# Output held by tokens, activations as the stationary operand, and the first experts' products in the last part of attention

## The reference

```python
x = L0_attn_x
xn = _layernorm(x, axis=-1)
x = x + _L0_attn_ref(xn, ...) + _L0_ffn_ref(xn, ...)
```

```python
g = jnp.einsum('th,eih->tei', x, w_gate_proj)     # 32 experts, inner size 96
u = jnp.einsum('th,eih->tei', x, w_up_proj)
h = jax.nn.silu(g) * u
h = h * masked_w[:, :, None]
out = jnp.einsum('tei,ehi->th', h, w_down_proj)
```

## Time and profile before

| | |
|---|---|
| median of 3 runs | 1143.94 us (1143.56 to 1144.35) |
| the profiled execution | 1144.08 us |
| its span, first to last instruction | 1142.3 us, mean granted clock 0.994 |
| TensorE matmul busy | 1106.8 us (97%), 7360 matmuls |
| TensorE weight loads busy | 911.9 us (80%), 7360 loads |
| VectorE, ScalarE, GpSimd busy | 739.5, 635.2, 490.8 us |
| moved by DMA | 67.85 MB, 59 GB/s over the span |

### The profile page before, as it was taken

How to read it: one execution, slowest core, us unless ns; L and a number is a source line. 1 busy time by engine, 2 the same in 40 slices (tenths; PEclk the granted TensorE clock), 3 DMA queues, 4 the chain that set the end, 5 groups by cost and what they waited for, 6 DMA issues and landing times. The chain is left out here.

```text
span 1142.3 us, 22436 instructions
## 1 busy us (share of the span) xinstructions
PE 1106.8 (97%) x7360; PEld 911.9 (80%) x7360; DVE 739.5 (65%) x1556; ACT 635.2 (56%) x1285; POOL 490.8 (43%) x384
## 2 busy tenths in 40 slices
PE   6989999999999999999999999899999999999997
PEld 3668888888888888888888887688888878888885
DVE  6878778678688687687787765454444445444444
ACT  3575766766766767667766676443434333343332
POOL 1265456466466456446546552033333332333332
PEclk9999999999999999999999999899999999999999
DMA  6100000000000000010000021273333334433332
GB/s 221 56 19 19 3 18 20 1 18 18 0 17 19 0 18 18 0 36 0 0 18 0 1 66 30 84 222 110 115 110 115 110 107 131 118 117 110 115 105 92
DMA packets 26309, 67.85 MB, mean 59 GB/s; under 512 B 3028, under 2 KB 9428, under 8 KB 26264
## 3 DMA queue, kind: packets, MB, share of 16 engines
q1 hardware_dynamic: 26120, 67.24, 19.5%
q10 hardware_dynamic: 144, 0.07, 0.0%
HBM read 62.82 MB, written 4.47 MB: 59 GB/s over the span
## 5 line engine op out<-in xcount | busy, mean ns | idle before, releaser
L838 ACT ACTIVATE prob<-ps_s,nm 128x128 f32<-128x128 f32 (+7 forms) x256 | 189.5, 740 | 164.8 <-DVE nm L998 162.9
L1436 POOL TENSOR_TENSOR hl<-hf,hh 128x512 fp32r<-128x512 f32 x96 | 123.4, 1286 | 295.4 <-ACT hh L1373 295.4
L998 DVE CUSTOM_DVE_ANT_0 ps_s<-ps_s,causal 128x128 f32<-128x128 f32 (+7 forms) x256 | 195.5, 764 | 55.0 <-PE ps_s L653 47.5
L664 PE MATMUL ps_t<-ident,prob 128*128 128x128 f32 x1152 | 177.5, 275 | 4.3 <-ACT pt L848 3.0
L664 PEld LDWEIGHTS ps_t<-ident,prob 128*128 128x128 f32 x1152 | 136.5, 140 | 30.4 <-issue 11.4
L679 PE MATMUL ps_o<-pt,kvn 128*64 128x128 f32 x2304 | 154.0, 278 | 0.5 <-DVE pt L1007 0.4
L679 PEld LDWEIGHTS ps_o<-pt,kvn 128*64 128x64 f32 x2304 | 123.2, 136 | 33.3 <-issue 21.3
L1405 DVE TENSOR_TENSOR gs<-gs,routing 128x512 f32<-128x512 f32 x64 | 44.3, 692 | 137.8 <-ACT gs L1369 137.8
L1007 DVE COPY pt<-ps_t 128x128 f32<-128x128 f32 (+2 forms) x192 | 102.0, 531 | 48.3 <-PE ps_t L664 46.4
L1373 ACT ACTIVATE hh<-hf 128x512 fp32r<-128x512 f32 x96 | 60.7, 633 | 121.6 <-DVE hf L1410 121.6
L1369 ACT ACTIVATE gs<-ps_g 128x512 f32<-128x512 f32 x96 | 57.4, 598 | 121.4 <-PE ps_g L1328 121.4
(11 more groups left out here) (291 smaller groups left out, 2560.2 us busy)
## 6 DMA issues: line engine op xcount, KB each, us to landing
routing<-wT_scratch SPq DMA_DIRECT2D x34, 256.0 KB, 3.7
raw_a<-in_e SPq DMA_DIRECT2D x17, 384.0 KB, 3.1
cosv<-in_e SPq DMA_DIRECT2D x17, 384.0 KB, 3.0
sinv<-wT_scratch SPq DMA_DIRECT2D x17, 384.0 KB, 3.6
raw<-in_e SPq DMA_DIRECT2D x17, 384.0 KB, 3.0
routing<-wT_scratch SPq DMA_DIRECT2D x16, 384.0 KB, 3.3
raw_a<-in_a SPq DMA_DIRECT2D x8, 512.0 KB, 3.3
raw_b<-in_b SPq DMA_DIRECT2D x8, 480.0 KB, 3.8
```

Source lines behind the costliest of these rows:

```text
L664: mm = nc.tensor.transpose(ps_t[x][:, at * P:(at + 1) * P], prob[t % 2][e][:, j * P:(j + 1) * P], ident[:, :])
L838: nc.scalar.activation(prob[t % 2][e][:, 0:len(halves) * width].rearrange("p (h k) -> p h k", k=width), ps_s[e][:, 0:len(halves), 0:width] ...
L998: nc.vector.tensor_tensor_reduce(out=s_ps, in0=s_ps, in1=bias, scale=-1.0, scalar=-MASKED, op0=ALU.add, op1=ALU.min, accum_out=nm[:, e:e + ...
L1436: nc.gpsimd.tensor_tensor(hl[:, c, :], hf[:, c, :], hh[:, c, :].bitcast(F32), ALU.subtract).then_inc(h_lo, 1)
```

## The change

The output `yacc` is held by tokens: 16 tiles of 128 tokens by 256 features. It is no longer cleared but loaded with x in `prepare`. In the output products and in the down products the activations (128 tokens) are stationary and the weights (256 features) move, so that results come out by tokens; `turn_back`, `xres`, `yout` and the residual add are gone, and the output is stored from `yacc` (the last round in four parts). Gate and up products have two banks each, the ones that held attention's scores. A round's second half of sums (`take_sums`) is added behind the next round's first unit. Tile 0's gate and up products for both units, the first unit's elementwise work and the second tile's weight split are issued in the last part of `attend`, and `mix` leaves them out. Weights, `gs`, `hf`, `hh`, `hl` lie in buffers of attention for this. In the last batch, the copy of the fourth group of routing weights moves ahead by one exponent, and the first expert's split by one block.

```diff
+            sp.dma_start(keep["yacc"][:, :, :], xv).then_inc(y_loaded, 16)
...
-            nc.gpsimd.memset(keep["yacc"][:, :, :], 0.0).then_inc(y_zeroed, 1)
-            pool.wait_ge(y_zeroed, 1)
...
+def gate_or_up(nc, keep, out, q, tokens, w0):
+
+    whi, wlo, xhi, xlo = keep["whi"][q], keep["wlo"][q], keep["xhi"], keep["xlo"]
+    for k in range(2):
+        cols = slice(w0 + k * P, w0 + (k + 1) * P)
+        nc.tensor.matmul(out[:, :], whi[:, cols], xhi[k][:, tokens], start=k == 0, stop=False)
+        nc.tensor.matmul(out[:, :], whi[:, cols], xlo[k][:, tokens], start=False, stop=False)
+        mm = nc.tensor.matmul(out[:, :], wlo[:, cols], xhi[k][:, tokens], start=False, stop=k == 1)
+    return mm
...
             def out_products(out, m):
-                cols = slice(m * P, (m + 1) * P)
-                nc.tensor.matmul(out[:, :], bhi[:, cols], ohi[:, :], start=True, stop=False)
-                nc.tensor.matmul(out[:, :], bhi[:, cols], olo[:, :], start=False, stop=False)
-                return nc.tensor.matmul(out[:, :], blo[:, cols], ohi[:, :], start=False, stop=True)
+
+                for h in range(2):
+                    tokens, cols = slice((2 * m + h) * P, (2 * m + h + 1) * P), slice(h * C, (h + 1) * C)
+                    nc.tensor.matmul(out[:, cols], ohi[:, tokens], bhi[:, :], start=True, stop=False)
+                    nc.tensor.matmul(out[:, cols], ohi[:, tokens], blo[:, :], start=False, stop=False)
+                    mm = nc.tensor.matmul(out[:, cols], olo[:, tokens], bhi[:, :], start=False, stop=True)
+                return mm
...
             values(s, 1, t - 1)
+            pe.wait_ge(keep["x_lo"], 2)
+            pe.wait_ge(keep["expert_lo"], 1)
+            pe.wait_ge(exp_done, s * U + 2 * t + 1)
+            gate_or_up(nc, keep, ps_s[0][:, 0, :], 0, slice(0, CH), 0).then_inc(keep["gate_ready"], 1)
             for g in range(2):
                 turn(s, t, 1, g)
             pe.wait_ge(widened, s * 2 + 2)
             pe.wait_ge(y_added, s * 4 + 2)
             spread(ps_x).then_inc(misc_ready, 1)
+            gate_or_up(nc, keep, ps_s[0][:, 1, :], 0, slice(0, CH), UP_AT).then_inc(keep["up_ready"], 1)
             values(s, 1, t)
+            gate_or_up(nc, keep, ps_s[1][:, 0, :], 0, slice(CH, 2 * CH), 0).then_inc(keep["gate_ready"], 1)
+            gate_or_up(nc, keep, ps_s[1][:, 1, :], 0, slice(CH, 2 * CH), UP_AT).then_inc(keep["up_ready"], 1)
             pe.wait_ge(olo_done, 2 * s + 2)
             for m, out in enumerate((ps_x, ps_t[0])):
                 out_products(out, m).then_inc(misc_ready, 1)
...
+                        if not more and t == 3:
+                            store_turned(i, b, t)
...
-                        if not more and t < 4:
+                        if not more and t < 3:
...
-                        if not more and t == TILES - 1:
+                        if not more and t == TPC + 2:
                             act.wait_ge(keep["w_loaded"][0], 16)
                             nc.scalar.activation(keep["whi"][0], keep["raw"][0], ACT.Copy).then_inc(keep["expert_hi"], 1)
...
+            def silu(c):
+                act.wait_ge(keep["gate_ready"], c + 1)
+                act.wait_ge(w_stored, 16 * (N // ROUND + 1))
+                nc.scalar.activation(keep["gs"][:, c, :], ps_s[c][:, 0, :], ACT.Silu).then_inc(keep["silu_done"], 1)
+            silu(0)
             out_hi(s, 1, BEFORE_LAST + len(LAST) - 1)
+            act.wait_ge(keep["w_loaded"][1], 16)
+            nc.scalar.activation(keep["whi"][1], keep["raw"][1], ACT.Copy).then_inc(keep["expert_hi"], 1)
+            silu(1)
+            act.wait_ge(keep["h_done"], 1)
+            nc.scalar.activation(keep["hh"][:, 0, :], keep["hf"][:, 0, :], ACT.Copy).then_inc(keep["h_hi"], 1)
...
-                at = slice(b * T + c * CH, b * T + (c + 1) * CH)
-                nc.vector.tensor_tensor(yacc[:, m, at], yacc[:, m, at], ps[:, :], ALU.add).then_inc(y_added, 1)
+                first = (b * T + c * CH) // P + 2 * m
+                held = yacc[:, first:first + 2, :].rearrange("p t c -> p (t c)")
+                nc.vector.tensor_tensor(held, held, ps[:, :], ALU.add).then_inc(y_added, 1)
...
+                        if not more and t == TILES - 1:
+                            dve.wait_ge(keep["expert_hi"], 1)
+                            nc.vector.tensor_tensor(keep["wlo"][0], keep["raw"][0], keep["whi"][0].bitcast(F32), ALU.subtract).then_inc(keep["expert_lo"], 1)
...
-            dve.wait_ge(keep["expert_hi"], 1)
-            nc.vector.tensor_tensor(keep["wlo"][0], keep["raw"][0], keep["whi"][0].bitcast(F32), ALU.subtract).then_inc(keep["expert_lo"], 1)
             normalise(s, 1)
+            gs, hf = keep["gs"], keep["hf"]
+            dve.wait_ge(keep["silu_done"], 1)
+            dve.wait_ge(keep["routing_loaded"][0], ROUTED)
+            nc.vector.tensor_tensor(gs[:, 0, :], gs[:, 0, :], keep["routing"][0][:, 0:CH], ALU.mult).then_inc(keep["gated"], 1)
             dve.wait_ge(ohi_done, s * 2 + 2)
             nc.vector.tensor_tensor(olo[:, :], on[:, :], ohi[:, :].bitcast(F32), ALU.subtract).then_inc(olo_done, 1)
-            for m, ps in enumerate((ps_x, ps_t[0])):
-                add_out(n + 1 + m, ps, s, 1, 1, m)
+            dve.wait_ge(keep["gated"], 1)
+            dve.wait_ge(keep["up_ready"], 1)
+            nc.vector.tensor_tensor(hf[:, 0, :], gs[:, 0, :], ps_s[0][:, 1, :], ALU.mult).then_inc(keep["h_done"], 1)
+            add_out(n + 1, ps_x, s, 1, 1, 0)
+            dve.wait_ge(keep["expert_hi"], 2)
+            nc.vector.tensor_tensor(keep["wlo"][1], keep["raw"][1], keep["whi"][1].bitcast(F32), ALU.subtract).then_inc(keep["expert_lo"], 1)
+            add_out(n + 2, ps_t[0], s, 1, 1, 1)
...
+            pool.wait_ge(keep["h_hi"], 1)
+            nc.gpsimd.tensor_tensor(keep["hl"][:, 0, :], keep["hf"][:, 0, :], keep["hh"][:, 0, :].bitcast(F32), ALU.subtract).then_inc(keep["h_lo"], 1)
...
-        ps_y = [[bank(f"ps_y{m}{c}") for c in range(UNITS)] for m in range(2)]
-        ps_g, ps_u, ps_t = bank("ps_g"), bank("ps_u"), [bank(f"ps_tr{k}") for k in range(2)]
+        ps_g, ps_u = ([keep["ps_s"][c][:, k, :] for c in range(UNITS)] for k in range(2))
+        ps_y = [[bank(f"ps_y{c}{k}") for k in range(2)] for c in range(UNITS)]
...
-                        sp.dma_start(xres[:, :, :], xv).then_inc(res_loaded, 16)
...
-                for m in range(2):
-                    cols = slice(DOWN_AT + m * P, DOWN_AT + (m + 1) * P)
-
-                    nc.tensor.matmul(ps_y[m][c][:, :], whi[q][:, cols], hh[:, c, :], start=first, stop=False, skip_group_check=True)
-                    nc.tensor.matmul(ps_y[m][c][:, :], whi[q][:, cols], hl[:, c, :], start=False, stop=False, skip_group_check=True)
-                    mm = nc.tensor.matmul(ps_y[m][c][:, :], wlo[q][:, cols], hh[:, c, :], start=False, stop=True, skip_group_check=True)
+                wide = slice(DOWN_AT, DOWN_AT + C)
+                for t in range(TPC):
+                    tokens, to = slice(t * P, (t + 1) * P), ps_y[c][t // 2][:, (t % 2) * C:(t % 2 + 1) * C]
+
+                    nc.tensor.matmul(to, hh[:, c, tokens], whi[q][:, wide], start=first and t % 2 == 0, stop=False, skip_group_check=True)
+                    nc.tensor.matmul(to, hh[:, c, tokens], wlo[q][:, wide], start=False, stop=False, skip_group_check=True)
+                    mm = nc.tensor.matmul(to, hl[:, c, tokens], whi[q][:, wide], start=False, stop=True, skip_group_check=True)
                 mm.then_inc(down_done, 1)
...
-            def turn_back(r, c):
-
-                pe.wait_ge(y_summed, r * 4 + 2 * c + 2)
-                for t in range(c * TPC, (c + 1) * TPC):
-
-                    ge(pe, y_final, r * TR + t - t % 2 - 2)
-                    for m in range(2):
-                        mm = nc.tensor.transpose(ps_t[t // 2 % 2][:, (t % 2) * C + m * P:(t % 2) * C + (m + 1) * P],
-                                                 yacc[:, m, r * ROUND + t * P:r * ROUND + (t + 1) * P], ident[:, :])
-                    mm.then_inc(y_transposed, 1)
...
-                            ge(pe, silu_done, n)
-                            for out_ps, w0, done in ((ps_g, 0, gate_ready), (ps_u, UP_AT, up_ready)):
-                                if done is up_ready:
-                                    ge(pe, h_done, n)
-                                for k in range(2):
-                                    cols = slice(w0 + k * P, w0 + (k + 1) * P)
-                                    nc.tensor.matmul(out_ps[:, :], whi[q][:, cols], xhi[k][:, tokens], start=k == 0, stop=False)
-                                    nc.tensor.matmul(out_ps[:, :], whi[q][:, cols], xlo[k][:, tokens], start=False, stop=False)
-                                    mm = nc.tensor.matmul(out_ps[:, :], wlo[q][:, cols], xhi[k][:, tokens], start=False, stop=k == 1)
-                                mm.then_inc(done, 1)
-
-                            if c:
```

(71 more changed lines are left out.)

45 lines of the change are left out of this document (16 added, 29 removed).

## The result

The changed kernel takes 1139.29 us (median of 7 runs, 1137.87 to 1140.29), the kernel before 1143.56 beside it: ratio 0.9966, 95% interval 0.9954 to 0.9977. By this ratio it is 0.3% faster; by the medians that is 4.3 us, half of the 8.7 that were forecast. The profiled execution took 1139.54 us for a span of 1137.8. Repeated beside the last two experiments the changed kernel took 1139.31, ratio 0.9982 (0.9969 to 0.9994). The two ratios differ because executions of the kernel before come in two groups by mean granted clock: of 17 beside that repetition, ten at 0.999 took 1140.3 to 1141.6 us and six at 0.994, the clock of the profile shown of before, 1143.6 to 1145.2; against the ten alone the change gives 1.4 us (medians 1140.67 and 1139.31).

A forecast was written before the change was run, and what follows sets the result against it. TensorE, busy without a gap in both long stages, was taken to bound the kernel. Gains of -15.0 and costs of +6.3 us gave -8.7 from 1144.08: 1135.4, or 1135.2 by the median; range 1130 to 1140, chance 0.72.

The forecast's parts named there:

- Down products: Expert stage: six 512-wide matmuls per unit become twelve of 256, costing 0 to 7.7 us; middle +3.8 taken.
- Output products: Attention: 64 calls, each three 512-wide matmuls becoming six 256-wide, costing 0 to 2.6 us; middle +1.2.
- Routing rows stored earlier: Attention's last pass, near 697 us: TensorE's wait for ScalarE's copy of the fourth group goes, -1.8 us.
- First products in attention's tail: End of attention and start of experts: early gate and up products fill TensorE's waits, -5.7 us.
- The clock there: End of attention and stage boundary: a possible fall of the granted clock, between 0 and +2.7; +1.3 us taken.
- The first routing rows: Expert stage opening: rows for unit 2's down product arrive just in time, covered by 0.1 us; 0 taken, +2 kept.
- Switch: Switch of rounds: second banks for gate and up remove two waits of TensorE, -2.1 us.
- Turning back: Expert stage: the first round's 16 transposes go, -2.6 us.
- The load of x: First stage: x loaded into the accumulator, 13.2 us to landing, covered by 30 us of work; uncovered up to 13.
- Tail: Kernel's end: last adds end at 1136.1 instead of 1138.93, the half-size store given its old time, -2.8 us.
- the one with both spacings at their upper end: Rival: down and output products at 120 ns per 256-wide matmul and the clock falls, 1142.0 us; chance 0.14.
- The feed and the loads: Two slower rivals: instruction feed limits TensorE, 1157.7 us, chance 0.06; weight loads bind the expert stage, 1172 us, chance 0.04.

The follow-up runs named there:

- the last two experiments: Two versions of the changed kernel with early routing rows and down products by features in the first round, the second also in half the second round: 1136.05 and 1133.95 us.
- the width taken back: Changed kernel with down products as six 512-wide matmuls, weights stationary, instead of twelve of 256, sums not turned back: 1129.99 us.
- the first experiment: Kernel before with each down product's matmul over 512 tokens issued as two over 256, weights still stationary: 1151.49 us, ratio 1.0075.
- the last version: Changed kernel with early routing rows and down products by features in the first round and the second round's first half of tokens: 1133.95 us, ratio 0.9928.
- the one before it: Changed kernel with early routing rows and down products by features in the first round alone, turned back in the second: 1136.05 us, ratio 0.9948.
- the run with 128 columns: Kernel before with each down product's matmul over 512 tokens issued as four over 128, weights stationary: 1278.99 us, one execution.

## Why the prediction was right or wrong

The step that failed is the term "Down products", +3.8 us; it measured 9.3 (the width taken back). Two things were wrong in it. First its value: of the ends 113.3 and 120 ns the middle was taken, since "neither end is nearer". The rows did decide. 226.7 ns at 512 and 120 at 256 lie 106.7 ns apart for 256 columns, 0.417 ns a column, which is one column per cycle at the upper level of 2.4 GHz; what is left, 13.3 ns, is by this line paid per matmul whatever the width, and so twice as often. The upper end was thus the one that fits both rows, and would have made 7.7 (7.1 by the spacings of the trace, where the first of each run takes 114). The line was measured between 256 and 512 columns only; at 128 it failed. The reason for the middle, that attention's 512-wide matmuls are slower, did not carry over to the short ones: they cost 120 ns in the expert stage as well. Second a part that no row of before could give a price to, because no run of 256-wide matmuls stood ahead of 512-wide ones in the expert stage: the slower five behind each run, 0.027 x 91 = 2.5 us. What makes these long ones slower stays open. The text's mark for being wrong, 4.2 us per unit, was too wide to show it. The other terms miss by +1.3 and +0.5 (routing rows, first products) on one side and by -1.3 (the clock), -0.8, -0.4, -0.3 and -0.3 on the other; that they nearly cancel is luck.

*Output products*: +1.2, measured +0.78, from the lengths of attention in executions without a fall of the clock near 50 us (633.16 in the first experiment, 633.90 to 633.96 in five runs with the new form). Right within 0.4 us. The two executions of the table both had that fall, which costs 1.5.

*Routing rows stored earlier*: -1.8, measured -1.91 and given back as +1.97. Right.

*First products in attention's tail*: -5.7. By its own points, from the `values` product to the first matmul of the expert stage and one down product of 1.4, the trace has 14.74 + 1.4 = 16.1 us for 15.65: -5.2. Right in the trace; but some 2.4 of it was the clock fall at the end of attention, as the first experiment shows, in whose profile the old tail had none and took 25.8 us for 28.15. In executions of the kernel before without that fall there is little to gain (25.8 to 24.6 in these traces), and the run without the early products shows as much.

*The clock there*: +1.3 was a middle of 0 and 2.7. In the profile it was 0. Of the eight traces with the early products in attention's tail, three have a fall of 3.4 us near the boundary, the repetition among them, and four have none there but one near 50 us; its price near the boundary is 1.6 where no wait hides it (24.62 us in the last version, 23.06 in the one before it) and 0.3 in the changed kernel (24.91 for 24.59), where the wait for the routing rows shrinks by as much.

*The first routing rows*: 0, and +2 kept. It measured +1.3. The rows were estimated to land near 739.4 and ended VectorE's wait at 740.3, while TensorE stood at the product at 742.5 instead of 743.1; a cover of 0.1 us does not bear such errors. The text's own mark for this, a wait of over 1 us in the first three units, was met.

*Switch*: -2.1, measured -2.07; the matmul at 935.68 in the earlier trace rows is the last of its six and not the first, but the 1.50 us lost behind it are right. *Turning back*: -2.6; the stretch of units 48 to 94 gives 1.75 - 46 x 0.10 = -2.9. *The load of x* took 17.2 us to landing instead of 13.2 and stayed covered. *Tail*: -2.8, measured -3.56: the last add comes 2.9 earlier, and the store behind it, which was given the old time, is half the size and takes 2.7 us for 3.4.

Of the rivals, the one with both spacings at their upper end was right for the down products, too high for the output products (0.8 for 2.6) and wrong for the profile in its clock. The feed and the loads did not bind at 256 columns: the loads' share rose from 132.5 to 141.3 of 160, not to 177, since they overlap. The Trainium skill (Perfetto Trace Analysis, "Identifying the Most-Contended Engine") names that share, beside the share of peak FLOPs (MFU), as a measure of how close TensorE is to its limit. Here it hardly tells: 132.5, 141.3 and, in the run with 128 columns, 144.5 of 160 us stand beside units of 4.08, 4.18 and 5.46.

## What to carry to other kernels

Two spacings at different widths give a line: look whether its slope is one column per cycle of the granted clock, and price every split by what the line leaves at width zero, before taking a middle; below the widths measured the line need not hold (it failed here at 128). A layout that saves a transpose at the end is paid for in the inner loop if it narrows the moving operand: here 9.3 us for the 6.5 of the turning back and the tail (2.9 + 3.6), and the better kernel keeps the wide form inside and transposes once per round, in banks that are idle and in a wait that exists. When work is moved into waits, add up the waits on both sides of the move (3.87 and 3.69 us here) before counting the work as gained.

## What the runs showed of the hardware

A 512-wide matmul behind two or more 256-wide ones is 1 to 14 ns slower (228 to 241 for 226.7), behind a run of twelve for five in a row, whatever is stationary; behind 24 of 128 columns the first one takes 0.29 us. At 128 columns a matmul with its load costs 112 ns, so that narrowing from 256 saves 8 ns, while a matmul of that width alone needs no more than 58. And the granted clock fell to 0.50 for 3.4 us in two executions of the changed kernel at two places, near 50 us in the one and behind the boundary in the other; the trace of the kernel before has a fall of 3.4 us near 50 and one of 6.8 us at the end of attention. That such falls alone make the two groups of the kernel before, 3.1 us apart in their medians, is likely but not shown, as the one trace of that kernel is of the group at 0.994.
